# First attention: a head's two output parts summed by a product on PE

## The reference, cut to what matters

```python
q = q.reshape(B, N, H, Dh); k = k.reshape(B, M, H, Dh); v = v.reshape(B, M, H, Dh)
scale = 1.0 / np.sqrt(Dh)                                   # Dh = 32
attn = jax.nn.softmax(jnp.einsum('bnhd,bmhd->bhnm', q, k) * scale, axis=-1)
o = jnp.einsum('bhnm,bmhd->bnhd', attn, v).reshape(B, N, C)
```

## Time and profile before

| what | value |
|---|---|
| median of three runs | 3331.55 us |
| the profiled execution, its own time | 3347.56 us |
| its span | 3345.8 us |
| PE, PEld, DVE, ACT, POOL busy in the span | 88%, 70%, 72%, 63%, 41% |
| first attention, from the first scores to the last output | about 215 to 590 us |

### The profile page before, as it was taken

The page is one execution under the profiler, slowest core; times in us unless marked ns, Lnnn a source line. Parts: engine busy times, 40 slices in busy tenths (PEclk is TensorE's granted clock), DMA queues, the critical chain, the costliest instruction groups (busy, mean ns, idle before and its releaser), DMA issues. The chain is left out here.

```text
span 3345.8 us, 57650 instructions
## 1 busy us (share of the span) xinstructions
PE 2955.3 (88%) x15511; PEld 2356.0 (70%) x15542; DVE 2409.5 (72%) x4802; ACT 2095.2 (63%) x4247; POOL 1359.2 (41%) x1667
## 2 busy tenths in 40 slices
PE   6848998588899969959999899999999999799677
PEld 4636666476788848748787778888888888687444
DVE  6759999665676657766676279999999999524387
ACT  3448888331566636546666488888888888322254
POOL 4400000513000047236676267777777777331131
PEclk9979999799899989979999999999999999899899
DMA  5776563413887759765656632222233222476200
GB/s 186 242 161 156 143 155 99 125 45 133 268 267 261 230 161 295 192 168 150 184 159 187 216 99 80 82 92 94 93 93 94 84 81 65 161 241 205 73 22 29
DMA packets 403247, 490.88 MB, mean 147 GB/s; under 512 B 36388, under 2 KB 251828, under 8 KB 403092
## 3 DMA queue, kind: packets, MB, share of 16 engines
q1 hardware_dynamic: 391140, 440.31, 44.3%
q0 software_dynamic: 11952, 48.78, 4.1%
HBM read 312.69 MB, written 176.31 MB: 146 GB/s over the span
## 5 line engine op out<-in xcount | busy, mean ns | idle before, releaser
L2808 POOL TENSOR_SCALAR h_probs<-h_exp,h_rowsum_inv 128x512 f32<-128x512 f32 x512 | 357.5, 698 | 273.9 <-PE h_pT L2656 256.4
L2736 DVE TENSOR_REDUCE h_neg_max<-h_scores 128x1 f32<-128x512 f32 x512 | 349.7, 683 | 141.6 <-PE h_scores L2648 141.2
L2698 ACT ACTIVATE h_exp<-h_scores,h_neg_max 128x512 f32<-128x512 f32 x512 | 356.2, 696 | 108.5 <-DVE h_neg_max L2736 100.6
L2749 DVE TENSOR_TENSOR h_probsT_lo<-h_pT,h_probsT_hi 128x512 fp32r<-128x512 f32 x512 | 348.8, 681 | 0.0
L2795 POOL TENSOR_TENSOR n_lo<-n_raw,n_hi 128x512 fp32r<-128x512 f32 x248 | 320.4, 1292 | 0.0
L2656 PE MATMUL h_pT<-ident,h_probs 128*128 128x128 f32 x2048 | 306.2, 272 | 0.9 <-POOL h_probs L2808 0.8
L2656 PEld LDWEIGHTS h_pT<-ident,h_probs 128*128 128x128 f32 x2048 | 252.9, 139 | 70.0 <-POOL h_probs L2808 2.4
L2707 ACT CAST h_probsT_hi<-h_pT 128x512 fp32r<-128x512 f32 x512 | 301.2, 588 | 0.9 <-PE h_pT L2656 0.9
L2402 PE MATMUL g_pQ<-g_w_hi,g_x 128*128 (+1 forms) x640 | 268.2, 419 | 29.1 <-DMA g_x<-xq 19.8
L2402 PE MATMUL g_pQ<-g_w_lo,g_x 128*128 (+1 forms) x640 | 255.1, 399 | 0.0
L2669 PE MATMUL h_pO<-h_probsT_hi,n_hi 128*128 128x512 f32 x512 | 244.3, 477 | 0.0
(11 more groups left out here) (419 smaller groups left out, 8430.2 us busy)
## 6 DMA issues: line engine op xcount, KB each, us to landing
e_w_raw<-in_w SPq DMA_DIRECT2D x24, 1792.0 KB
lnT<-g_out SPq DMA_DIRECT2D x160, 256.0 KB, 2.3
n_raw<-lnT SPq DMA_DIRECT2D x64, 512.0 KB, 5.3
e_w_raw<-in_w SPq DMA_DIRECT2D x24, 896.0 KB
b_q_stack<-qk SPq DMA_DIRECT2D x64, 256.0 KB
b_k_stack<-qk SPq DMA_DIRECT2D x64, 256.0 KB
xq<-f_out SPq DMA_DIRECT2D x16, 1024.0 KB, 6.8
g_x<-xq SPq DMA_DIRECT2D x64, 256.0 KB, 3.3
```

The lines of the kernel that those rows point to most:

```text
L2698: nc.scalar.activation(Pr[:, r % 4], pS[r % 2][:], ACT.Exp, bias=nmax[:, r % 4:r % 4 + 1], accum_out=rsum[:, r % 4:r % 4 + 1]).then_inc(ex ...
L2736: v.tensor_reduce(nmax[:, r % 4:r % 4 + 1], pS[r % 2][:], axis=AX, op=ALU.max, negate=True).then_inc(nmax_done.sem, 1)
L2749: v.tensor_tensor(PTl[:, br * HPG + h, :, bass.ts(q, P)], pT[r % 4][:], PTh[:, br * HPG + h, :, bass.ts(q, P)], ALU.subtract).then_inc(lo_ ...
L2808: nc.gpsimd.tensor_scalar(Pn[:, r % 4], Pr[:, r % 4], rinv[:, r % 4:r % 4 + 1], 1.0, ALU.mult, ALU.mult).then_inc(norm_done.sem, 1)
```

## The change

In the first attention `o_transposes` multiplies each 64 x 128 block of oT by `ident_pair`, a 64 x 32 matrix of two identities, one below the other. The result, 128 x 32, is already the sum of the two parts. pR shrinks from 64 to 32 columns per block, the reduce and its tile o_sum go, and DVE's multiply reads pR in PSUM. The constants stage writes the new matrix.

```diff
+                nc.gpsimd.memset(g["ident_pair"][:], 0.0).then_inc(s_zero, 1)
+                pool.wait_ge(s_zero, 4)
+                for k in range(2):
+                    nc.gpsimd.affine_select(out=g["ident_pair"][:], in_=g["ident_pair"][:], compare_op=ALU.not_equal, fill=1.0,
+                                            base=-k * DH0, pattern=[[-1, DH0]], channel_multiplier=1).then_inc(s_zero, 1)
+                    pool.wait_ge(s_zero, 5 + k)
...
-        osum = m.sb("o_sum", [P, 2, QT, DH0])
...
-        pR = m.ps("pR", [P, QT, 2 * DH0])
+        pR = m.ps("pR", [P, QT, DH0])
...
                 for k in range(QT):
-                    last = nc.tensor.transpose(pR[:, k], Os[:, h % 2, bass.ts(k, P)],
-                                               g["ident"][0:2 * DH0, 0:2 * DH0])
+                    last = nc.tensor.matmul(pR[:, k], Os[:, h % 2, bass.ts(k, P)], g["ident_pair"][:], start=True, stop=True)
                 last.then_inc(oTr_done.sem, 1)
...
-                link = Links(dve, dve_link, nh, 2)
+                link = Links(dve, dve_link, nh, 1)
                 dve.wait_ge(o_done.sem, o_done.free(nh))
                 link(nc.vector.reciprocal(rinv[:, h % 2], rsum[:, h]))
                 dve.wait_ge(oTr_done.sem, oTr_done.done(nh))
-                link(nc.vector.tensor_reduce(osum[:, h % 2], pR[:].rearrange("p k (w c) -> p k c w", w=2),
-                                             axis=AX, op=ALU.add))
                 if h == 0:
                     dve.wait_ge(o_out[gb], 16 + i * 16)
-                nc.vector.tensor_tensor(O[:, gb, :, h * DH0:(h + 1) * DH0], osum[:, h % 2],
+                nc.vector.tensor_tensor(O[:, gb, :, h * DH0:(h + 1) * DH0], pR[:],
                                         rinv[:, h % 2].unsqueeze(2).to_broadcast([P, QT, DH0]),
                                         ALU.mult).then_inc(o_done.sem, 1)
...
+        "ident_pair": nc.alloc_sbuf_tensor("ident_pair", [2 * DH0, DH0], F32),
```

More of the change, by code:

```diff
@@ L176, in _ @@
                 nc.gpsimd.memset(g["neg_half"][:], -0.5).then_inc(s_zero, 1)
-                pool.wait_ge(s_zero, 3)
+                nc.gpsimd.memset(g["ident_pair"][:], 0.0).then_inc(s_zero, 1)
[4 more added lines that the diff above has]
+                    pool.wait_ge(s_zero, 5 + k)
                 for idt in (g["ident"], g["ident16"]):
@@ L180, in _ @@
                                             base=0, pattern=[[-1, P]], channel_multiplier=1).then_inc(s_zero, 1)
-                pool.wait_ge(s_zero, 5)
+                pool.wait_ge(s_zero, 8)
             @block.scalar
```

## The result

The changed kernel took 3376.81 us in the median (3375.09 to 3383.22, 4 runs), the kernel before 3334.18 us beside it; the ratio is 1.0131, with a 95% interval of 1.0119 to 1.0143. It is slower, as forecast, but by 42.6 us where 30.9 were forecast, and its time lies 0.8 us above the end of the range. A later comparison gave 3376.28 against 3340.98 us, ratio 1.0106 (1.0089 to 1.0123): there the difference is 35.3 us. In the profiled executions the spans differ by less, 3374.6 against 3345.8: 28.8 us.

What follows compares the result with a forecast made beforehand. The first attention's ring through PE and ACT, 5.83 us per head, was taken as the bound. 34.7 - 2.8 - 1.2 + 0.15 = +30.9 us on 3331.55 gave 3362.4 us, range 3341 to 3376.

Steps and rivals of the forecast that it cites:

- The ring, and pR as its link by occupation: First attention: copy oT, pR, transposes, ACT's `high` form a 5.83 us ring per head; pR counts by occupying PE.
- The size of pR: PE's products take 0.89 to 0.96 us against 0.39; 0.55 more per head, 34.7 us over 63 intervals.
- The multiply: DVE's multiply from PSUM takes 0.29 us and starts 1.18 after pR, `low` at 1.39, each 0.15 later.
- The two disturbed heads: A turn's first unit gains 0.40 us, 2.8 in all; the loop's branch 0.18 to 0.2, 1.2 in all.
- Sum of the stage: First attention: 34.7 - 2.8 - 1.2 + 0.15 = +30.9 us.
- All other stages at nothing: Outside the first attention: constants cost 0, queue, DMAs and engine order the same, all other stages as before.
- Quick loads: PE's products: loads from 64 partitions go 0.06 us apart, 0.24 more per head; +11 us, 3342; chance 0.10.
- loads without overlap: PE's products: load and product don't overlap, 0.88 us more per head; +51 us, 3383; chance 0.08.
- one pair per product: PE's time comes out even, each float32 product one load and matmul, or hidden; 3327 to 3339 us; chance 0.06.
- DVE as the bound: First attention: each head gives back the reduce's 0.46 us, 29 us in all; 3302 us; chance 0.04.

Runs made afterwards that it cites:

- `no_reduce`: Kernel before without DVE's reduce, the multiply reading the first 32 columns of each block of pR; 3336.23 us, ratio 0.9988.
- `rows128`: Changed kernel with oT and the matrix extended by zeros to 128 partitions; 3361.11 us, ratio 1.0075 to the kernel before.
- The square: Four kernels, first to last copy oT: transposes and reduce 368.4 us, transposes alone 363.6, products and reduce 407.0, products alone 402.3.
- `before_again`: Kernel before, unchanged, run for a second profile; 3342.43 us, ratio 1.0001.
- `before_moved`: Kernel before with o_transposes right behind the next unit's transposes and ahead of its scores, normalise at lag 11; 3357.13 us, ratio 1.0058.
- `before_late`: Kernel before with o_transposes between scores and values, normalise at lag 14, row sums kept for eight heads; 3321.59 us, ratio 0.9966.
- `late128`: Kernel before given products over 128 partitions, between scores and values, matrix in the attention's own scope, no reduce; 3303.12 us, ratio 0.9902.
- `const_only`: Kernel before with the new matrix written in the constants stage but not used; 3347.34 us, ratio 1.0018.
- `pad_only`: Kernel before with the new matrix's 128 bytes per partition set aside and never written; 3341.17 us, one run.
- `after_again`: Changed kernel again, unchanged, on the same chip as its parts; 3376.28 us, ratio 1.0106 to the kernel before.

## Why the prediction went wrong, point by point

- **The ring, and pR as its link by occupation.** Right. The links of an ordinary head are unchanged but for pR, and `no_reduce` shows DVE beside it.
- **The size of pR.** The first failed step and the smaller one, a term mis-sized. Count (two matmuls and loads per product) and pace (0.11 apart) were right. "0.50 to 0.57 us more per head. I take 0.55" measured 0.618, and 0.60 in the distance of the copies; over 63 intervals 37.8 us where 34.7 were counted. The gap behind the last load is 0.23, not 0.11 to 0.18: I had put what I saw of it before down to a stall, and with 128 partitions in `rows128` it is 0.03. The square gives 38.6 us for the products.
- **The multiply.** Right: starts at 1.18 and `low` at 1.39 after pR, the multiply from PSUM 0.29.
- **The two disturbed heads.** Right: 0.45 gained in the first unit's (0.40 forecast), 0.21 in the branch's (0.18 to 0.2); the square gives 4.7 us, 4.0 were forecast.
- **Sum of the stage.** 33.9 us measured (35.7 by the second pair of traces), 30.9 forecast. This step misses 3.0 of the 11.7 us between forecast and measured difference.
- **All other stages at nothing.** The second failed step and the larger: 8.7 us of the measured difference arose there. "SP's queue, the DMAs and the order on every engine stay the same" is true, but a new fixed tile moves every later one. The second attention, from first to last exponential, became 2.5 us longer (930.0 to 932.5), and 3.1 or 3.2 in the two kernels that have the tile alone.
- **The rest.** 33.9 + 2.5 = 36.4 us, ratio 1.0109. It lies in the second comparison's interval and below the first's (39.7 to 47.7 us by its ratio), so 6.2 us of the first are not located. The runs taken together say that most of this too comes with the tile. Take from each kernel's difference to the median before what its copies oT gained or lost against 368.4. In the kernels without the fixed tile -1.4 to 1.8 us is left (`before_again`, `no_reduce`, `before_moved`, `before_late`, `late128`). In seven of the eight that have it 6.4 to 11.1 us is left (`const_only` 6.8, `pad_only` 8.6), only `after_again` having -0.3. Each figure by itself is uncertain by several us, as the intervals of the ratios are. As an estimate from all thirteen, the tile costs some 7 us, of which the second attention shows 3; where the other 4 arise stays open. The profiled pair can't show it: there `l0_output` was 6.1 us shorter after the change (228.4 to 222.3), but it was 222.0 in `pad_only`, 231.5 in the second profile of before and 217.0 in `before_late`.
- **The distance to the range.** The prediction added its sum to 3331.55 us, the lowest of the medians that the kernel before had: 3331.55 (3 runs), 3334.18 (4), 3340.98 (24), 3338.53 (7) and 3333.12 (14). That is 2.6 of the 14.4 us by which the measured time lies above 3362.4. In the second comparison the difference of 35.3 us is within the forecast's +24 to +37. That the first time fell 0.8 us outside the range and not inside is partly chance; the two failed steps aren't.
- **The rivals.** Quick loads, loads without overlap, one pair per product and DVE as the bound all failed: the first two by the pace of 0.11, the third by the count of 512, the last by `no_reduce`. The rule of the Trainium skill ("TensorE: Matmul & The Clock Gate", section "LDWEIGHTS (loading the stationary operand)") that a load goes by columns and not by rows held over 64 partitions: loads 0.11 apart over 64 and over 128. The 81 ns per pair of the Trainium skill (same page, section "Back-to-back issue gap") did not show here: the pairs stood 112 ns apart.

## What to carry to other kernels

In a ring of engines an instruction costs by the time it occupies its engine ahead of what others wait for, so look for the place where its engine waits anyhow, and check every consumer of what is pushed back, not only the one that waits now. A transpose replaced by a plain float32 product had twice the loads here, and each was slower; a product that has half the partitions of its neighbours paid at both edges, and here rows of zeros were cheaper. A new tile belongs in the scope that uses it, lest all later tiles move. Where the changed stage doesn't account for the total, compare what is left over all the kernels that share a feature.

## What the runs showed of the hardware

- PE took 0.29 us less per head when pR's products used 128 partitions instead of 64 between neighbours of 128: 0.326 to 0.232 us from the matmul ahead to its first, 0.133 to 0.028 from its first to its second, 0.203 to 0.112 from its last to the next group's first.
- A float32 product of 32 columns ran as two matmuls with two loads of 128 columns, 0.11 us apart (512 of each for 256 products); a transpose as one, its load 0.06 us behind the last.
- 128 bytes per partition of unused memory among the fixed tiles made the loads of the second attention's transposes 141 ns instead of 139, and the stage some 3 us longer; all eight traces that have them show 58.7 us for 32 units, all six that lack them 58.5.
